# Two edits to the last feed-forward of a fused transformer kernel: unsplit down weights, and shared chunks among the routing steps

## What is computed

```python
scores = jax.nn.sigmoid(x @ gate_w)
topk_w, topk_i = jax.lax.top_k(scores, TOP_K)               # 6 of 32 experts
topk_w = topk_w / (jnp.sum(topk_w, axis=-1, keepdims=True) + 1e-20)
...
g = jnp.einsum('td,edf->tef', x, wg)                        # 96 hidden per expert
u = jnp.einsum('td,edf->tef', x, wu)
act = jax.nn.silu(g) * u
routed = jnp.einsum('tef,efd,te->td', act, wd, combine)
shared = jax.nn.silu(hidden_states @ sg) * (hidden_states @ su) @ sd    # 192 hidden
return routed + shared
```

## Time and profile before

| what | value |
|---|---|
| time, median of 3 runs | 1303.89 us (1302.59 to 1307.35) |
| span of the profiled execution, first to last instruction | 1495.7 us |
| time of the profiled execution itself | not recorded; it can't be under its span |
| mean granted TensorE clock, profiled execution | 0.865 |
| PE busy | 1178.6 us (79%) |
| DVE, ACT, POOL busy | 743.8, 536.0, 596.8 us |
| tiles of f = 2, first to last matmul of line 910 | 794.5 to 995.1 us |
| tiles of f = 3, the same | 1261.6 to 1473.9 us |

### The profile page before, as it was taken

The page is one execution under the profiler, slowest core; times in us unless marked ns, Lnnn a source line. Parts: engine busy times, 40 slices in busy tenths (PEclk is TensorE's granted clock), DMA queues, the critical chain, the costliest instruction groups (busy, mean ns, idle before and its releaser), DMA issues.

```text
span 1495.7 us, 20198 instructions
## 1 busy us (share of the span) xinstructions
PE 1178.6 (79%) x6031; PEld 960.0 (64%) x6031; DVE 743.8 (50%) x2333; ACT 536.0 (36%) x1012; POOL 596.8 (40%) x579
## 2 busy tenths in 40 slices
PE   4799988979989898854768998897755436988884
PEld 4677755666778676633557987875434225978784
DVE  5553465564546536413445555678644214633443
ACT  2323344554533234321413433442303115644442
POOL 3661352211124213674550155662453730045554
PEclk9789999998989999865868999898875667998897
DMA  9523439400002573331426687760121212676676
GB/s 331 211 72 107 143 96 308 141 1 0 1 29 107 206 260 119 117 114 64 173 76 216 195 241 237 219 191 4 60 79 41 105 53 63 198 208 205 204 223 191
DMA packets 125302, 209.81 MB, mean 140 GB/s; under 512 B 15296, under 2 KB 104768, under 8 KB 123328
## 3 DMA queue, kind: packets, MB, share of 16 engines
q1 hardware_dynamic: 100624, 141.38, 28.7%
q0 software_dynamic: 24576, 67.14, 14.4%
HBM read 129.29 MB, written 101.19 MB: 154 GB/s over the span
## 4 chain that ended last, share of the span: by engine, by line
PE 48%; DVE 18%; issue 13%; another core or an unknown queue 10%; ACT 6%; POOL 3%; DMA 1%; SPq 0%; DVEq 0%; POOLq 0%; ACTq 0%
PE ps L910 15%; PE ps L932 6%; PE ps L877 5%; PE ps L817 4%; PE ps L829 4%; PE ps L889 3%; PE ps L1093 2%; PE ps L1100 2%; ACT xnt L1360 1%; PE ps L927 1%; PE ps L1244 1%; DVE HL L2047 1%; POOL xd L638 1%; PE ps L925 1%
## 5 line engine op out<-in xcount | busy, mean ns | idle before, releaser
L653 POOL DMA_INDIRECT G<-yd,slot_of x256 | 253.1, 989 | 424.6 <-issue 189.3
L638 POOL DMA_INDIRECT xd<-xnt,slot_of x256 | 251.4, 982 | 224.4 <-DVE slot_of L1986 136.9
L910 PE MATMUL ps<-WE,xT 128*128 x1016 | 200.7, 343 | 5.6 <-issue 3.9
L2102 DVE TENSOR_TENSOR hid<-hid,ps 128x192 f32<-128x192 f32 (+2 forms) x168 | 65.4, 389 | 247.9 <-ACT hid L1551 198.1
L910 PEld LDWEIGHTS ps<-WE,xT 128*128 128x128 f32 x1016 | 174.0, 202 | 9.9 <-issue 9.7
L1522 ACT ACTIVATE xT<-ps 128x512 f32<-128x512 f32 (+1 forms) x168 | 99.2, 590 | 156.9 <-PE ps L877 121.6
L877 PE MATMUL ps<-ident,xd_in 128*128 128x128 f32 x664 | 108.2, 287 | 44.2 <-ACT xT L1522 24.0
L2081 DVE SCALAR_TENSOR_TENSOR XT<-G,wt,XT 128x256 f32<-128x256 f32 x256 | 123.8, 494 | 27.5 <-DMA G<-yd,slot_of 17.0
L1551 ACT ACTIVATE hid<-ps 128x192 f32<-128x192 f32 (+2 forms) x168 | 60.4, 359 | 192.1 <-PE ps L910 139.9
L877 PEld LDWEIGHTS ps<-ident,xd_in 128*128 128x128 f32 x664 | 84.5, 148 | 60.6 <-issue 37.0
L1379 ACT ACTIVATE S<-ps 128x512 f32<-128x512 f32 (+1 forms) x72 | 42.6, 592 | 179.1 <-PE ps L817 140.1
(11 more groups left out here) (245 smaller groups left out, 2173.6 us busy)
## 6 DMA issues: line engine op xcount, KB each, us to landing
xd_in<-xd SPq DMA_DIRECT2D x164, 256.0 KB
yd<-yo SPq DMA_DIRECT2D x164, 256.0 KB
WE<-w SPq DMA_DIRECT2D x8, 1280.0 KB
W0E<-w0e SPq DMA_DIRECT2D x1, 4864.0 KB
xd<-xnt,slot_of POOLq DMA_INDIRECT x256
G<-yd,slot_of POOLq DMA_INDIRECT x256
W0E<-w0e SPq DMA_DIRECT2D x1, 3040.0 KB
XT<-x_in SPq DMA_DIRECT2D x4, 512.0 KB, 6.1
```

The lines of the kernel that those rows point to most:

```text
L638: nc.gpsimd.indirect_dma_start(xd[f // 2][:, :], bass.IndirectOffsetOnAxis(ap=slot_of[:, t, k:k + 1], axis=0), xnt[:, t, :], None).then_in ...
L653: nc.gpsimd.indirect_dma_start(G[:, n % G_RING, :], None, yd[f // 2][0:min(ly.early[t][k] * 2, ly.TILES) * P, :], bass.IndirectOffsetOnAxi ...
L910: last = mm(dst, xT[:, q % 2, a, k, :], flat[:, bass.ds(expert[2 * q + a] + k * 2 * ly.H, 2 * ly.H)], start=(k == 0), stop=(k == KD - 1))
L2102: tt(hid[:, q % 2, 0:m, 0:ly.H], hid[:, q % 2, 0:m, 0:ly.H], src, ALU.mult).then_inc(TL.hid, 1)
```

## The change

It does four things, all in f = 3.

1. The down matmul of f = 3 becomes the plain float32 one of f = 2. `down_high`, `down_back`, `down_low` and `h_low3` go, with their buffers, semaphores, the second list of expert offsets (emap2, `hi_regs`) and the waits on them in `up`, `hturned` and `down_rows`.
2. S3 and HL3 move to the start of the attention weights' space, XH[3, 3] to that of XF, XH[3, 2] to that of QT. Nothing of the shared chunks lies in the space of xd_in any more, and SP's wait for `CK.sum` before `tiles(3)` goes. PE's stays.
3. In `window`, shared chunks stand between the routing steps of blocks 2 and 3, on PE, ACT and DVE.
4. The chunks of blocks 0 and 1 of f = 3 both use PSUM banks 2 and 3, so that the other pair is left to the transposes.

The last three hunks are PE's, ACT's and DVE's parts of `window`, in this order.

```diff
-            add(("s", f, b), ("s1", "s3")[f - 2], f, b, SH1, (2, 6))
+            add(("s", f, b), ("s1", "s3")[f - 2], f, b, SH1, (2, 6) if f == 2 or b >= 2 else (2, 2))
...
-        inside, upto = area(ring_at)
-        WDH = inside("WDH", [P, E1, D], F32R)
-        XH[3, 2] = inside("XH3_2", [P, 2, KD, BT], F32R)
+        inside, upto = area(r1_at)
+        HL3 = inside("HL3", [P, 2, 2, BT], F32R)
+        S3 = inside("S3", [P, 2, BT], F32)
+        upto[0] = qt_at - 4 * KD * D - 4 * 2 * KD * BT
         XH[3, 3] = inside("XH3_3", [P, 2, KD, BT], F32R)
...
+        XH[3, 2] = sb("XH3_2", [P, 2, KD, BT], F32R, qt_at)
...
             tiles(2, attention_weights)
-            sp.wait_ge(CK.sum, GROUP["s", 3, 3] + 1)
             tiles(3)
...
                 def hturned(q):
...
-                    if f == 3:
-                        pe.wait_ge(TL.hlo, HALVED0 + q - q0)
...
                 def up(q):
...
-                    if f == 3 and i == 1:
-                        pe.wait_ge(ew_lo, PARTS0 + 8)
...
                 def down_rows(q):
...
-                    if f == 3:
-                        if q == q0:
-                            pe.wait_ge(ew_lo, PARTS0 + 8)
-                        pe.wait_ge(TL.hlo, HALVED0 + q - q0 + 1)
-                        for a in range(ly.tiles_in(q - q0)):
-                            dst, n = ps[:, ty, a * D:(a + 1) * D], ly.part
-                            hi = whi[0:n, bass.ds(high_at[2 * q + a], D)]
-                            mm(dst, hTp[0:n, q % 2, 0, a, :], hi, start=True, stop=False)
...
                     for a in range(ly.tiles_in(q - q0)):
                         for c in range(ly.parts):
                             last = mm(ps[:, ty, a * D:(a + 1) * D], hT[0:ly.part, q % 2, a * ly.parts + c, :],
...
             def window():
...
+                def chunk(k):
+                    gate_up(chunks[k], taken_over(chunks[k]))
+                    if k:
+                        down(chunks[k - 1])
...
                 pe.wait_ge(A1.add, 8)
-                gate_up(chunks[0], taken_over(chunks[0]))
+                chunk(0)
                 logits_of(2)
                 next_turn(3)
                 next_rank(2)
+                chunk(1)
                 logits_of(3)
+                chunk(2)
+                next_rank(3)
                 pe.wait_ge(F_NORM[3].lo, NB)
-                gate_up(chunks[1], taken_over(chunks[1]))
-                down(chunks[0])
-                next_rank(3)
-                for i in range(2, len(chunks)):
-                    gate_up(chunks[i], taken_over(chunks[i]))
-                    down(chunks[i - 1])
-                    if i == 3:
+                for k in range(3, len(chunks)):
+                    chunk(k)
+                    if k == 5:
                         expert_row(3, A_BANK)
...
                 split_high(2)
+                silu(chunks[0])
                 score(3, 2, A_BANK + 1)
                 rows(F_NORM[3], 3, XT[:, tiles_of(3), :])
+                hidden(chunks[0])
                 plain(3)
                 split_high(3)
+                silu(chunks[1])
                 score(3, 3, A_BANK + 1)
-                for i, ch in enumerate(chunks):
+                hidden(chunks[1])
+                for ch in chunks[2:]:
                     silu(ch)
                     hidden(ch)
-                    if i % 2:
-                        down_high(i // 2)
-                    if i >= 3:
-                        down_back(i - 3)
-                for g in (5, 6, 7):
-                    down_back(g)
...
                 chosen(f, 2)
+                prod(chunks[0])
+                low_hidden(chunks[0])
                 slots(f, 2, A_BANK)
                 split_low(3)
+                prod(chunks[1])
                 chosen(f, 3)
-                prod(chunks[0])
-                low_hidden(chunks[0])
+                low_hidden(chunks[1])
+                finish(chunks[1])
+                prod(chunks[2])
                 slots(f, 3, A_BANK)
-                for i in range(1, len(chunks)):
+                low_hidden(chunks[2])
+                for i in range(3, len(chunks)):
                     prod(chunks[i])
                     low_hidden(chunks[i])
-                    if i == 3:
+                    if i == 5:
                         experts(f, A_BANK)
                     if chunks[i].last:
                         finish(chunks[i])
-                    if i >= 3:
-                        down_low(i - 3)
-                for g in (5, 6, 7):
-                    down_low(g)
```

More of the change, by code:

```diff
@@ L32 @@
 X2_RING = 3
-PARTS0 = 0
-HALVED0 = 0
 class Layer:
@@ L418, in __init__ @@
                 self.hT = sem("tl_hT")
-                self.hlo = sem("tl_hlo")
                 self.down = sem("tl_down")
@@ L789, in expert_row @@
                 pe.wait_ge(RT.ecol, f + 1)
-                if f == 3:
-                    mm(ps[0:1, bank, P:2 * P], ecol[:, 14:15], ident[:, :], start=True, stop=True)
                 mm(ps[0:1, bank, 0:P], ecol[:, 13:14], ident[:, :], start=True, stop=True).then_inc(RT.erow, 1)
@@ L849, in _ @@
             regs = [[pe.alloc_register(f"expert{g}_{i}") for i in range(4)] for g in range(2)]
-            hi_regs = [[pe.alloc_register(f"high{g}_{i}") for i in range(4)] for g in range(2)]
-            expert, high_at = {}, {}
+            expert = {}
             def next_experts(f, q):
@@ L856, in next_experts @@
                 pe.load(regs[g], emap[0:1, 2 * i:2 * i + 4])
-                if f == 3:
-                    pe.load(hi_regs[g], emap2[0:1, 2 * i:2 * i + 4])
-                    for r in range(4):
-                        high_at[2 * q + r] = pe.snap(hi_regs[g][r], min_val=0, max_val=(LAYER[f].E - 1) * D)
                 for r in range(4):
@@ L917, in down_rows @@
                     ty = down_bank(f, q)
-                    if f == 3:
-                        if q == q0:
-                            pe.wait_ge(ew_lo, PARTS0 + 8)
-                        pe.wait_ge(TL.hlo, HALVED0 + q - q0 + 1)
-                        for a in range(ly.tiles_in(q - q0)):
-                            dst, n = ps[:, ty, a * D:(a + 1) * D], ly.part
-                            hi = whi[0:n, bass.ds(high_at[2 * q + a], D)]
-                            mm(dst, hTp[0:n, q % 2, 0, a, :], hi, start=True, stop=False)
-                            mm(dst, hTp[0:n, q % 2, 0, a, :], wlo[0:n, bass.ds(expert[2 * q + a] + ly.down_at, D)], start=False, stop=False)
-                            last = mm(dst, hTp[0:n, q % 2, 1, a, :], hi, start=False, stop=True)
-                        last.then_inc(TL.down, 1)
-                        return
                     for a in range(ly.tiles_in(q - q0)):
@@ L1495, in prepare2 @@
                     chunk(k)
-            def down_high(g):
-                if g == 0:
-                    act.wait_ge(CK.gu, RUN["s", 3, 0][0][-1].i + 1)
-                    act.wait_ge(A1.add, 8)
-                fn(WDH[:, 8 * g:8 * g + 8, :], WDR[:, 8 * g:8 * g + 8, :], ACT.Copy).then_inc(ew_hi, 1)
-            def down_back(g):
-                act.wait_ge(ew_hi, g // 2 + 1)
-                if g:
-                    act.wait_ge(ew_lo, g)
-                else:
-                    act.wait_ge(RT.emap, 4)
-                fn(ps[:, A_BANK:A_BANK + 2, :].rearrange("p a n -> p (a n)"), WDH[:, 4 * g:4 * g + 4, :].bitcast(F32).rearrange("p e n -> p (e n)"),
-                   ACT.Copy).then_inc(ew_back, 1)
             def tiles(f, beside=None, between=None):
@@ L1528, in hturned @@
                     n_h = ly.tiles_in(q - q0) * ly.parts * P
-                    if f == 3:
-                        fn(hTp[0:ly.part, q % 2, 0].rearrange("p a t -> p (a t)")[:, 0:n_h], ps[0:ly.part, hth, 0:n_h], ACT.Copy).then_inc(TL.hT, 1)
-                        return
                     fn(hT[0:ly.part, q % 2].rearrange("p a t -> p (a t)")[:, 0:n_h], ps[0:ly.part, hth, 0:n_h], ACT.Copy).then_inc(TL.hT, 1)
@@ L2012, in experts @@
                 dve.wait_ge(RT.erow, f + 1)
-                if f == 3:
-                    copy(emap2[0:1, 0:2 * LAYER[f].PAIRS], ps[0:1, bank, P:P + 2 * LAYER[f].PAIRS])
                 copy(emap[0:1, 0:2 * LAYER[f].PAIRS], ps[0:1, bank, 0:2 * LAYER[f].PAIRS]).then_inc(RT.emap, 1)
@@ L2109, in rows @@
                     copy(yo[:, q % Y_RING, 0:m].rearrange("p a d -> p (a d)"), ps[:, down_bank(f, q), 0:m * D]).then_inc(TL.y, 1)
-                def h_low3(q):
-                    dve.wait_ge(TL.hT, q + 1)
-                    if q >= 2:
-                        dve.wait_ge(TL.down, q - 1)
-                    n = ly.tiles_in(q - q0) * P
-                    part = lambda v: hTp[0:ly.part, q % 2, v].rearrange("p a t -> p (a t)")[:, 0:n]
-                    tt(part(1), ps[0:ly.part, 2, 0:n], part(0).bitcast(F32), ALU.subtract).then_inc(TL.hlo, 1)
                 for q in range(q0, q1):
@@ L2124, in tiles @@
                         between(q - q0)
-                    if f == 3:
```

(15 more changed lines are left out.)

17 lines of the change are left out of this document (1 added, 16 removed).

## The result

| | time, us | against the kernel before |
|---|---|---|
| before, 20 runs | 1302.13 (1296.93 to 1307.63) | |
| changed kernel, 20 runs | 1307.36 (1304.5 to 1311.43) | ratio 1.0041, 95% interval 1.0027 to 1.0054 |
| forecast | 1311 (1294 to 1318), slower 0.40, within 0.5% 0.36 | +7.2 us |

What follows compares the result with a forecast made beforehand. It took POOL's scatters to set the start of f = 3's tiles and PE to bound the tiles: +9.3 (down matmul) - 2 (start) - 0.4 (last pair) + 0.3 (block 2) = +7.2 on 1303.9, giving 1311 us, range 1294 to 1318.

Steps and rivals of the forecast that it cites:

- What bounds the start: Start of f = 3's tiles: POOL's scatters allow `up` at 1197, shared chunks and split at 1200.4, meeting within 3 us.
- the redone clock: Profile times in `window` recomputed without the five long unexplained waits, 61.2 us in all.
- a gain of 3, which I take as 2: Start of f = 3's tiles: removing the split ends the chunks' side by about 1190, leaving POOL's 1197; counted -2 us.
- Down matmul, +9.3: Tiles of f = 3: float32 form costs 0.150 us more per pair, over 62 pairs, +9.3 us.
- Window order: `window`: `slots` of block 3 comes up to 11.7 us later, still covered by POOL's 30.3 us of work; cost 0.
- +0.3 for block 2: `slots` of block 2 in `window`, behind a `prod` and a `low_hidden` on DVE: +0.3 us, if POOL is idle then.
- SP's wait and buffers: Loads before f = 3's tiles run ahead of the chunks: 0 with POOL last, up to 3 us if chunks are last.
- R1: Start of f = 3's tiles: chunks were last by more than thought, whole split and SP's 3 us gained; 1305, chance 0.17.
- R2: `window`: unexplained waits under POOL's scatters are real in timed runs, chunks behind the last scatter set the path; 1296, chance 0.20.
- R3: `window`: `slots` of block 3 loses its cover, POOL idles 2 to 7 us, tiles start later; up to 1318, chance 0.08.
- R4: Tiles of f = 3: POOL's gathers, not PE, set most pairs' period; float32 costs 3 instead of 9.3, 1305, chance 0.10.
- The table loads: ACT in `window`: three more loads, 3.8 us, at most the one before block 2's scores on the chain.

Runs made afterwards that it cites:

- e1: Kernel before, unchanged, timed and profiled a second time: 1303.13 us, profile span 1301.0 us.
- e8: Kernel before with 64 instead of 96 scatters in f = 3: 1294.40 us, ratio 0.9937 to before.
- e5: Kernel before, window still making the split and tiles waiting for it, but with the plain float32 down matmul and no `h_low3`: 1308.55 us, ratio 1.0057.
- e6: Kernel before without `down_back` and `down_low`, all three float32r matmuls reading the high part: 1299.24 us, ratio 0.9985.
- e2: Kernel before with only the float32 down matmul and no split work; buffers, SP's wait, banks and window order as before: 1307.9 us, ratio 1.0050.
- e3: Kernel before with only the new window order and PSUM banks, split kept but moved behind the chunks: 1302.03 us, ratio 1.0007.
- e4: Changed kernel with SP's wait for the last shared chunk put back before the tiles of f = 3: 1307.52 us, ratio 1.0051 to before.
- e7: Changed kernel with 64 instead of 96 scatters in f = 3: 1283.53 us, ratio 0.9856 to before.
- e9: Unsplit float32 kernel in old window order with SP's wait (e2), with 64 instead of 96 scatters in f = 3: 1293.51 us, ratio 0.9935 to before.
- e10: Kernel before with two float32r down matmuls instead of three in f = 3, low part of the weights left out: 1295.11 us, ratio 0.9948.

## Why the prediction was right, and where it was not

The result, 1307.36, lies inside the range and 0.6 us under its likely part (1308 to 1315). The direction was that of the forecast, and so was the part that decides, the down matmul. The mechanism at the start was not, and that the sum still fits is in part luck: 1.4 us too much in the tiles and 1.5 us too much gain at the start cancel. Another 1.8 us of the distance to 1311 is the starting point, 1303.89 of three runs against 1302.13 of twenty. Step by step:

- **What bounds the start.** The forecast put POOL's chain at 1197 and the chunks' side at 1200.4 after taking the five long waits out. On POOL's side the first load is 1.5 us behind the last scatter and `up` some 7 to 8 behind its end, in both kernels, as stated; but POOL does not idle for the 7 us that the redone clock gives it ahead of block 2's scatters. In e1 it is 4.6 us behind when `slots` of block 2 is there, in the changed kernel 3.6. The chunks' side was not near: in e1 the last `finish` is over 8.6 us before the last scatter's issue and the last `down_low` 0.4 us before it, each well before SP's load, and e8 puts it 6 to 7 us ahead of POOL's, not 3 behind. The step "on the redone clock ... a gain of 3, which I take as 2" is the one that failed: nothing waited for the split, 0.5 was seen, and e5 and e6 tie that to the form of the tiles. Taking only the waits of the chain out of a disturbed profile did not give the undisturbed one: outside `window` too its stretches were longer (the tiles of f = 3 took 211.8 us, e1's 168.6). The clock row that was read as 0.9 or more in most slices has that in 19 of 40.
- **Down matmul, +9.3.** Pairs 2.677 to 2.826 us, as stated. Over all pairs it came to +7.9 in the profiles of e1 and the changed kernel. Some 0.7 us of the rest are periods of e1 that last 2.7 to 3.0 us here and there, before the gathers begin as well as in them, where the changed kernel's stay at 2.83; some 0.8 are the first and last two periods, which hardly differ between the kernels. The end behind the last `up` is 0.8 us shorter where 0.4 was taken.
- **Window order.** "Still covered" was right with far more room: `slots` of block 3 is 1.0 us later against block 2's, not 11.7, so most of PE's and ACT's parts must run beside DVE's, and POOL's free point comes 18 us later. The +0.3 for block 2 was 0, as POOL was not idle then. e2 and e3 show the order at zero from both sides.
- **SP's wait and buffers:** 0 with POOL last (e4), some 1.6 us where the wait would hold the load back (e7 against e9); forecast 0 and up to 3.
- **The rivals.** R1 (chunks last) and R2 (waits real) fell with e1: in e1 the chunks end 8.6 us before the last scatter, and no long wait is there. (R2's five chunks at 4.7 us should read 4.5, 5.7 less 1.2.) R3 didn't happen. R4 (PE not the bound in the gathers) fell for this change, as PE is idle 0.2 us of 115 in e1; one matmul lower, in e10, it idles 5.65.

The table loads cost nothing in the end, as forecast. Timeline of ACT in the changed kernel, those of blocks 2 and 3:

```profile
1021.61 1.28 ACT L1348 ACT_TABLE_LOAD   x1
1022.91 0.59 ACT L1348 ACTIVATE S<-ps 96x512 f32<-96x512 f32 x1
1023.52 1.28 ACT L1342 ACT_TABLE_LOAD   x1
1024.81 0.28 ACT L1342 ACTIVATE sc<-ps 128x128 f32<-128x128 f32 x1
...
1031.58 1.28 ACT L1348 ACT_TABLE_LOAD   x1
1035.02 0.59 ACT L1348 ACTIVATE S<-ps 96x512 f32<-96x512 f32 x1 [2.16 <-PE ps L804]
1035.63 1.28 ACT L1342 ACT_TABLE_LOAD   x1
1039.00 0.28 ACT L1342 ACTIVATE sc<-ps 128x128 f32<-128x128 f32 x1 [2.09 <-PE ps L1230]
```

The last two are over 2.16 and 2.09 us before ACT goes on, when PE has the operand ready. The first two ACT does pay for, but `slots` of block 2, which hangs on the score behind them, is still 3.6 us ahead of POOL. A drain of 1.38 us, as the Trainium skill has it (ScalarE: Activation LUTs, What ACT_TABLE_LOAD costs), would have fitted into the gaps of the last two. At the first two there is none of it: the silu follows the load at 1021.61 by 0.02 us, the next load the silu by 0.02 and the score that load by 0.01, as in the earlier trace rows.

So the parts that the change touches come to +7.9 in the tiles, -0.8 behind them and -0.5 ahead of them, +6.6, and the timed 5.2 (by the interval 3.5 to 7.0), 5.7 to 7.1 in e2, e4 and e5, agree with that.

## What to carry to other kernels

When a stage ends on a chain that one engine issues at a fixed pace (here 96 scatters at 1.265 us), look first whether that engine ever idles; if not, work taken off the others beside it gains nothing, however much it is, and what it costs elsewhere is paid in full. The same edits were worth 10.9 us as soon as a third of the chain was gone, so an edit must be judged again after each change of the bound. And a profile whose span is 15% over the timed runs should be taken again before a margin of a few us is read from it.

## What the runs showed that was not expected

- One execution of the kernel before spent some 190 us more under the profiler, 61 of them in five waits in `window` that lay where POOL issued scatters, 43 in the tiles of f = 3; the second profile of the same kernel had none of the five, with a span of 1301.0 us.
- A plain float32 matmul in place of three float32r ones costs 0.15 us a pair of tiles. Float32r matmuls of 256 columns follow one another by 0.118 us, six of them 0.71, where the float32 ones take 0.86.
- With two float32r matmuls the pair period stopped at 2.53 us in the median, before the gathers as during them. The matmuls gave the expected 0.12 us each; in every second pair, that in which PE's program loads the next experts' offsets, `up` gave 0.2 us of it back. The cause of that is open.
- With 32 of 96 scatters gone POOL's chain ended only 23.3 us earlier, as POOL then had to wait for `slots` of block 2.
